# Two transformer layers in one kernel: spilling q and k of layer 1 one by one, and other places in the slots

## The reference, cut to what matters

```python
x = L0_attn_query
xn = _layernorm(x)
x = x + L0_attn(xn) + L0_ffn(xn)      # 16 heads of 128, causal mask; gated gelu FFN in float8
xn = _layernorm(x)
x = x + L1_attn(xn) + L1_ffn(xn)      # 16 heads of 16, no mask; Hadamard-rotated silu FFN, hidden 1024

# L1_attn:
q = (x @ Wq + bq).reshape(b, l, 16, 16)
k = (x @ Wk + bk).reshape(b, l, 16, 16)
v = (x @ Wv + bv).reshape(b, l, 16, 16)
a = softmax(einsum('blhd,bLhd->bhlL', q, k) / 16)
out = einsum('bhlL,bLhd->blhd', a, v).reshape(b, l, 256) @ Wo + bo
```

## Time and profile before

| | |
|---|---|
| median of 3 runs | 989.36 us |
| the profiled execution: its time, its span | 987.0 us, 985.2 us |
| mean granted TensorE clock | 0.934 |
| busy: PE, DVE, ACT, POOL | 84%, 76%, 70%, 48% |
| a batch in the middle, in TensorE's windows | 95 to 97 us |

### The profile page before, as it was taken

How to read it: one execution, slowest core, us unless ns; L and a number is a source line. 1 busy time by engine, 2 the same in 40 slices (tenths; PEclk the granted TensorE clock), 3 DMA queues, 4 the chain that set the end, 5 groups by cost and what they waited for, 6 DMA issues and landing times.

```text
span 985.2 us, 21114 instructions
## 1 busy us (share of the span) xinstructions
PE 828.4 (84%) x7054; PEld 610.3 (62%) x7120; DVE 745.0 (76%) x2028; ACT 691.2 (70%) x1973; POOL 469.6 (48%) x734
## 2 busy tenths in 40 slices
PE   3456538999899999999899999999999999897564
PEld 1123225787677777777677777777777777665342
DVE  6988847766778877787778777877787887775584
ACT  2555616556678788877777888788778877785573
POOL 1443333313236655555555455556555555456342
PEclk9676769999999999999999999999999999999795
DMA  9544321212234344645464554455436454644454
GB/s 334 182 139 128 107 93 45 52 42 42 46 93 105 76 104 116 108 81 107 100 106 76 109 108 105 76 121 100 104 76 134 87 100 76 127 81 92 107 108 106
DMA packets 283178, 100.96 MB, mean 102 GB/s; under 512 B 241344, under 2 KB 281024, under 8 KB 281920
## 3 DMA queue, kind: packets, MB, share of 16 engines
q1 hardware_dynamic: 280368, 97.27, 44.3%
q10 hardware_dynamic: 2704, 2.36, 0.7%
HBM read 30.38 MB, written 10.49 MB: 41 GB/s over the span
## 4 chain that ended last, share of the span: by engine, by line
PE 52%; DVE 15%; SPq 8%; ACT 4%; issue 3%; DMA 3%; POOL 0%; POOLq 0%; DVEq 0%; ACTq 0%
PE ps L665 32%; PE ps L714 7%; SPq L1268 4%; PE ps L814 3%; PE ps L797 3%; PE ps L690 3%; DVE arena L659 2%; DVE arena L658 2%; DMA arena<-scratch_qk 2%; DVE arena L997 2%; DVE nb L1004 2%; SPq L1242 2%; ACT arena L873 2%; PE ps L823 1%; PE ps L799 1%
## 5 line engine op out<-in xcount | busy, mean ns | idle before, releaser
L659 DVE SCALAR_TENSOR_TENSOR arena<-ps,bqk,arena 128x256 bf16<-128x256 f32 x416 | 187.3, 479 | 71.2 <-ACT arena L654 70.1
L665 PE MATMUL ps<-arena,wqkv 128*128 128x256 bf16 x1728 | 215.5, 275 | 6.5 <-PEq L210 6.5
L654 ACT ACTIVATE arena<-ps,bqk 128x256 bf16<-128x256 f32 x416 | 179.4, 466 | 33.6 <-PE ps L665 23.1
L1172 POOL TENSOR_SCALAR arena<-arena,rc 128x128 f32<-128x128 f32 (+1 forms) x256 | 106.3, 428 | 184.0 <-DVE rc L1020 184.0
L665 PEld LDWEIGHTS ps<-arena,wqkv 128*128 128x128 bf16 x1728 | 161.7, 98 | 46.2 <-issue 28.1
L873 ACT ACTIVATE arena<-arena,nb 128x128 f32<-128x128 f32 (+1 forms) x256 | 114.3, 447 | 100.2 <-DVE nb L997 100.1
L1179 POOL TENSOR_SCALAR arena<-arena,rc 128x256 f32<-128x256 f32 x256 | 119.8, 483 | 84.9 <-DVE rc L1024 84.5
L1163 POOL TENSOR_TENSOR arena<-arena 128x512 bf16<-128x512 f32 x107 | 123.9, 1158 | 74.1 <-ACT arena L653 74.1
L653 ACT ACTIVATE arena<-arena 128x384 bf16<-128x384 f32 (+1 forms) x256 | 135.6, 568 | 13.6 <-POOL arena L1179 6.9
L873 ACT ACTIVATE arena<-ps,nb 128x256 f32<-128x256 f32 x256 | 118.8, 474 | 19.2 <-DVE arena L658 10.3
L714 PE MATMUL ps<-wo,arena 128*128 128x256 bf16 x768 | 106.5, 275 | 15.9 <-DVE arena L659 15.6
(11 more groups left out here) (98 smaller groups left out, 1279.6 us busy)
## 6 DMA issues: line engine op xcount, KB each, us to landing
arena<-scratch_qk SPq DMA_DIRECT2D x96, 64.0 KB, 2.2
arena<-arena SPq DMA_TRANSPOSE x256, 2.7
scratch_qk<-arena SPq DMA_DIRECT2D x32, 128.0 KB, 2.0
arena<-in_x SPq DMA_DIRECT2D x4, 512.0 KB, 8.8
arena<-in_w_gating SPq DMA_DIRECT2D x2, 1024.0 KB, 7.0
arena<-in_w_q SPq DMA_DIRECT2D x2, 1024.0 KB, 8.8
scratch_xT<-arena ACTq DMA_DIRECT2D x8, 256.0 KB, 6.5
arena<-in_w_k SPq DMA_DIRECT2D x2, 1024.0 KB, 6.4
```

Of the source, the lines that this page charges most:

```text
L654: return nc.scalar.activation(out, in_, ACT.Identity, bias=bias)
L659: return nc.vector.scalar_tensor_tensor(out=out, in0=in_, scalar=bias, in1=hi, op0=ALU.add, op1=ALU.subtract)
L665: last = nc.tensor.matmul(out, lhsT, rhs, start=(n == 0), stop=(n == len(steps) - 1))
L1172: last = nc.gpsimd.tensor_scalar(v, v, rc0[:, n % 4, i:i + 1], 1.0, ALU.mult, ALU.mult)
```

## The change

Six edits, all in the order of the slots' work or in who waits for what.

1. `spill` and `stack` take q (w = 0) and k (w = 1) one by one, with semaphores of their own. q is spilled in +8 and stacked in +9, k spilled in +9 and stacked in +10 (before: both spilled in +9 and stacked in +10).
2. In SP's slot they stand ahead of the turning DMAs, not behind them.
3. TensorE and ScalarE do transpose_x1 and the pieces behind `proj_v0` and `up_gate`, VectorE the low parts of both behind `v0_low` and `hidden`.
4. The v piece moves from +10 to +11.
5. VectorE's `variance` stands behind `max_0` and `o0_low` in its slot, not ahead.
6. ScalarE's high copy of q (or k) waits for the spill of q (or k) of the batch before alone.

```diff
-            return start1(b) + ((7, 8, 10)[w] if b < LASTB else 6)
+            return start1(b) + ((7, 8, 11)[w] if b < LASTB else 6)
...
                 if h == 0:
-                    pe.wait_ge(stacked[b % 2], 192 * (b // 2 + 1))
+                    for w in range(2):
+                        pe.wait_ge(stacked[w][b % 2], 96 * (b // 2 + 1))
...
@@ pe_program, the slot loop
+                if v_in(s) is not None:
+                    proj_v0(v_in(s))
+                for n in hidden_in[s]:
+                    up_gate(n, s)
                 for b in turns_in[s]:
                     transpose_x1(b)
                 for n in pieces_in[s]:
                     proj_qkv1(n)
-                if v_in(s) is not None:
-                    proj_v0(v_in(s))
-                for n in hidden_in[s]:
-                    up_gate(n, s)
...
@@ act_program
-                        act.wait_ge(spilled[(b - 1) % 2], 64 * ((b - 1) // 2 + 1))
+                        act.wait_ge(spilled[w][(b - 1) % 2], 32 * ((b - 1) // 2 + 1))
...
@@ dve_program, the slot loop
-                for b in ln_in[s]:
-                    variance(b)
                 if 0 <= s - 1 < NG0:
                     max_0(s - 1)
                 if 0 <= s - 4 < NG0:
                     o0_low(s - 4)
+                for b in ln_in[s]:
+                    variance(b)
...
-                for b in turns_in[s]:
-                    x1T_low(b)
-                for n in pieces_in[s]:
-                    qkv1_low(n)
                 for b in x1_in[s]:
                     x1_sum(b)
                 if v_in(s) is not None:
                     v0_low(v_in(s))
                 for n in hidden_in[s]:
                     hidden(n)
+                for b in turns_in[s]:
+                    x1T_low(b)
+                for n in pieces_in[s]:
+                    qkv1_low(n)
...
@@ sp_program
-            def spill(b):
-                sp.wait_ge(qkv1_lo, 3 * b + 2)
+            def spill(b, w):
+                sp.wait_ge(qkv1_lo, 3 * b + w + 1)
                 if b:
-                    sp.wait_ge(stacked[(b - 1) % 2], 192 * ((b - 1) // 2 + 1))
...
+                    sp.wait_ge(stacked[w][(b - 1) % 2], 96 * ((b - 1) // 2 + 1))
+                for a in range(2):
+                    sp.dma_start(scratch[w, a].rearrange("(m p) t -> p m t", p=P),
+                                 qk1[:, a, w, :, :]).then_inc(spilled[w][b % 2], 16)
+
+            def stack(b, w):
+                sp.wait_ge(spilled[w][b % 2], 32 * (b // 2 + 1))
                 upto(sp, s1_ps, H1 * (b - 1))
...
             for s in range(SLOTS):
+                for n in pieces_in[s - 1]:
+                    if n % 3 < 2:
+                        spill(*divmod(n, 3))
+                for n in pieces_in[s - 2]:
+                    if n % 3 < 2:
+                        stack(*divmod(n, 3))
                 if 0 <= s - 2 < NG0:
                     turn0(s - 2)
```

More of the change, by code:

```diff
@@ L630, in build @@
         turned1 = [sem(f"turned1_{i}") for i in range(RPT1)]
-        rows_ready, spilled, stacked = ([sem(f"{n}{i}") for i in range(2)] for n in ("rows_ready", "spilled", "stacked"))
+        rows_ready = [sem(f"rows_ready{i}") for i in range(2)]
+        spilled, stacked = ([[sem(f"{n}_{w}{i}") for i in range(2)] for w in "qk"] for n in ("spilled", "stacked"))
         stored = sem("stored")
@@ L973, in act_program @@
                     exp_1(n)
+                if v_in(s) is not None:
+                    v0_high(v_in(s))
+                for n in hidden_in[s]:
+                    gate_tanh(n)
                 for b in turns_in[s]:
@@ L977, in act_program @@
                     qkv1_high(n)
[L978 to L981, removed]
                 fold(s)
@@ L1250, in load_tokens @@
                              ).then_inc(cur_ready[b % 2], 16)
-            def spill(b):
-                sp.wait_ge(qkv1_lo, 3 * b + 2)
+            def spill(b, w):
+                sp.wait_ge(qkv1_lo, 3 * b + w + 1)
                 if b:
-                    sp.wait_ge(stacked[(b - 1) % 2], 192 * ((b - 1) // 2 + 1))
[L1256 to L1262, removed]
-                upto(sp, s1_ps, H1 * (b - 1))
[L1264 to L1270, removed]
+                    sp.wait_ge(stacked[w][(b - 1) % 2], 96 * ((b - 1) // 2 + 1))
[4 more added lines that the diff above has]
+                sp.wait_ge(spilled[w][b % 2], 32 * (b // 2 + 1))
+                upto(sp, s1_ps, H1 * (b - 1))
+                for r, a in enumerate(((0, 0, 1), (0, 1, 0))[w]):
+                    for par in range(2):
+                        row = 64 * par + HD1 * r
+                        sp.dma_start((qs, ks)[w][row:row + HD1, b % 2, :, :],
+                                     scratch[w, a].rearrange("(s e d) t -> e d s t", e=2, d=HD1)[par]
+                                     ).then_inc(stacked[w][b % 2], 16)
             def store(b):
@@ L1288, in sp_program @@
                     load_rows(b - 1)
[L1289 to L1294, removed]
                 for n in y_in[s - 1]:
```

## The result

| | before | after |
|---|---|---|
| median of 4 runs, us | 989.73 (988.39 to 990.41) | 958.84 (957.28 to 959.41) |
| ratio, 95% interval | | 0.9702 (0.9681 to 0.9722) |
| profiled execution: time, span, us | 987.0, 985.2 | 958.63, 956.8 |
| mean granted TensorE clock | 0.934 | 0.937 |

What follows compares the result with a forecast made beforehand. TensorE was taken to bound the middle batches, its waits costing their full length. Gains of 23.7 us in the middle and 6.7 in the last batch, 30.4 in all, gave 959.0 us, range 954 to 971.

Steps and rivals of the forecast that it cites:

- rival A: Whole kernel: all gains come as summed, 959 us, own range 955 to 964; chance 0.61.
- Edits 1 and 2: Middle batches: stacking DMAs issued earlier in SP's queue end TensorE's stack waits, gain 11.5 us, bounds 0 and 11.5.
- the slow clock's 3.3: Middle batches: the slower TensorE clock behind two stalls above 2.3 us goes with them, gain 3.3 us.
- Rival C: Stack waits: late through transfers, not place in SP's queue, so most of that gain is missing; 979 us, chance 0.07.
- Edits 3 and 4: Middle batches: waits ahead of x1's transposes (+6) and the v piece (+10) go, gains 3.6 and 2.7 us.
- the new wait in +9: Slot +9, ahead of project_out0: edit 3 adds about 0.17 us per batch, bounds 0 and 0.5; 1.0 over six.
- Edit 5: Slot +4: variance behind o0_low shortens project_out0's wait, gain 4.1 us over six batches, bounds 0 and 5.6.
- the 0.1 that was to come back a slot later: Slot after +4: about 0.1 us of edit 5's gain per batch lost again, VectorE having little idling to make up.
- batch 0: First batch: without scores1 or down as cover loses about 0.9 us, gets 0.4 back at its stack wait: -0.5.
- The last batch: Last batch: stack right behind SP's sixth turning DMA, 0.7 from slot +5; second exp gains 6.7 us, bounds 4 and 8.4.
- B: Whole kernel: new waits take a good part, 1 us in each of six batches and more; 970 us, chance 0.25.
- D: SP's queue in +9 and +10: turn0 gets behind spill and stack, misses attend0; slower, 1007 us, chance 0.05.

Runs made afterwards that it cites:

- z_sp_alone: Kernel before with edits 1, 2 and 6 alone, each turning DMA replaced by three plain copies that don't turn; 973.43 us, ratio to before 0.9862.
- m_port2: Small separate kernel: three kinds of VectorE instruction alone, then each beside a GpSimd add of two SBUF inputs; one execution of 72.16 us.
- z_last_old: z_after with the last batch's x1 transpose and its high and low parts ahead of up_gate again; 964.15 us, ratio to before 0.9769.
- z_after: The changed kernel with each turning DMA replaced by three plain DMAs copying the same bytes unturned; 967.36 us, ratio to before 0.9799.

## Why the prediction was right, and where it was not

The forecast of 959.0 met 958.84, and rival A came about. That the two agree to 0.2 us is partly luck. The span was forecast at 954.8 and came out at 956.8: the middle gave 3.2 us more than said and the last batch 5.2 less. And the median of before lay 2.7 above its profiled execution and that of after only 0.2, where the forecast carried 2.4 over, which makes up the 2.0.

**Edits 1 and 2: right.** All 11.5 us of stack waits went, and the slow clock's 3.3 with them: the longest idle time left in the middle is 0.9 and the granted clock 1.00. Slots +9 to +11 ran as worked out but for the stack of q, which took 3.81 us (half of 5.74 forecast), that of k taking 2.90; the margin at the scores came out at almost 4 us, and turn0 was never late. z_sp_alone shows that these edits, with edit 6, suffice. Rival C is refuted: the stacking DMAs take a median of 2.2 us to land before and after. Of the rule of the Trainium skill in "DMA: Bandwidth & Descriptors", section "Issuing engines are not separate DMA queues", that issue is usually small beside the DMA, the rows agree for one DMA (0.48 beside 2.2 to land). It doesn't carry over to twelve in a row, which hold SP for 5.74: the transfers are the same as before, only their place in the queue of issues has changed, and the waits are gone.

**How the terms are measured.** The list of the earlier trace rows gives the idle time between two records. That leaves out short waits, and where a record is missing it counts work as waiting. So the terms are measured here from the start of one instruction to the start of the next, against the same pair where nothing waits.

**Edits 3 and 4: right, and the new wait in +9 came.** Ahead of the transposes the wait had cost 0.77 us by this measure (0.60 in the list) and ahead of the v piece 0.61 (0.45), so the two gave 4.6 and 3.7 for 3.6 and 2.7. The new wait in +9 is not in the list, but it is there. VectorE's o0_low of after, TensorE's project_out0 in +9 and +10, and the weight load of the first:

```profile
452.31 0.48 DVE L660 SCALAR_TENSOR_TENSOR arena<-ps,bqk,arena 128x256 bf16<-128x256 f32 x1
```

```profile
451.30 1.48 PE L666 MATMUL ps<-arena,wqkv 128*128 128x256 bf16 x12
452.84 0.83 PE L716 MATMUL ps<-wo,arena 128*128 128x256 bf16 x6
...
456.88 1.48 PE L666 MATMUL ps<-arena,wqkv 128*128 128x256 bf16 x12
458.20 0.82 PE L716 MATMUL ps<-wo,arena 128*128 128x256 bf16 x6
```

```profile
452.84 0.55 PEld L716 LDWEIGHTS ps<-wo,arena 128*128 128x128 bf16 x6 [0.34 <-DVE arena L660]
```

o0_low ends at 452.79 and project_out0 starts at 452.84, 1.54 us after the product ahead of it. In +10 it is 1.32, so 0.22 is lost, and it is 0.22 or 0.23 in each of the six batches: 1.4 us where I had 0.17 each and 1.0.

**Edit 5: right in +4, 4.7 for 4.1.** The weight loads ahead of project_out0 in +4, before and then after:

```profile
425.28 0.10 PEld L669 LDWEIGHTS ps<-zeros 128*128 128x128 bf16 x1
426.50 0.55 PEld L714 LDWEIGHTS ps<-wo,arena 128*128 128x128 bf16 x6 [1.11 <-DVE arena L659]
```

```profile
422.19 0.55 PEld L716 LDWEIGHTS ps<-wo,arena 128*128 128x128 bf16 x6 [0.34 <-DVE arena L660]
```

A matmul on zeros stands ahead of project_out0 there, in both kernels. In the trace of before its record is missing in +4, so the 0.94 of the earlier trace rows holds some 0.2 us of work; z_sp_alone, where nothing of edit 5 is in and the record is there, lists 0.72. From the start of the product to that of project_out0 it took 2.43 us before (424.07 to 426.50) and takes 1.65 after (420.55 to 422.20): 0.78 less, what variance had held VectorE for. A little wait stays, as said: o0_low ends at 422.15 and project_out0 starts at 422.20. Only the 0.1 that was to come back a slot later did not.

Moving variance also shortened it. Its last instruction and the GpSimd instruction beside it, before:

```profile
424.91 0.59 DVE L1086 TENSOR_SCALAR ve<-mv 128x2 f32<-128x2 f32 x1
...
424.81 0.68 POOL L1184 TENSOR_TENSOR arena<-arena 128x256 bf16<-128x256 f32 x1 [1.58 <-DVE arena L1067]
```

The same two of after:

```profile
422.33 0.17 DVE L1088 TENSOR_SCALAR ve<-mv 128x2 f32<-128x2 f32 x1
...
421.28 0.67 POOL L1186 TENSOR_TENSOR arena<-arena 128x256 bf16<-128x256 f32 x1 [1.58 <-DVE arena L1069]
```

Before, the 128x2 instruction started beside GpSimd's and took 0.59 us; after, GpSimd's had ended at 421.95, and it took 0.17. Its median over eight batches went from 586 to 170 ns, and m_port2 shows the same stretching by itself. In +4 that changes nothing, for a stretched instruction holds VectorE like a long one. It may be why the 0.1 did not come back; no run shows that.

The sum of the middle then closes: 11.9 for the stack by this measure, 3.3 for the slow clock, 4.6, 3.7 and 4.7, less 1.4 in +9, is 26.8, against 26.9 measured. That leaves 0.1 for batch 0, where I had a loss of 0.5. So the middle was under-sized by 3.2, mostly because the list shows each wait some 0.1 to 0.2 too short.

**The last batch: right in its mechanism, wrong in one step.** The failed step is "Another 0.7 comes from slot +5, where up_gate now fills the 0.63 that the transposes waited". That wait did go, but slot +5 lost 3.0 us: the scores of slot 132 come 26.86 us earlier than before, the pieces (908.82 before, 884.95 after) only 23.87. I had followed the transposes to what they wait for, and not to who waits for them. Right behind them stands attend1, which takes the bank BK_M when x1T_low has let it go. Before, the twelve matmuls of up_gate lay between and covered ScalarE and VectorE; now they lie ahead and cover nothing. z_last_old shows it: the old order in that slot gives 3.65 us back up to the first stacked scores, 1.9 of them by the start of the pieces. z_sp_alone, with the new queue and the old order, has no wait ahead of attend1. How much of the 2.81 is the order and how much the long cast no run tells apart; the cast's excess is 1.1. In the middle batches the same order costs nothing, as attend1 isn't in slot +6 or +7 there.

The rest went as worked out. SP's sixth turning DMA ended at 893.64, 22.9 earlier than before, where 23.9 were left after slot +5; the stack followed at once, and the scores came 7.6 us after its start (7.5 forecast):

```profile
892.40 1.24 SPq L1244 DMA_TRANSPOSE arena<-arena  x1
893.73 5.74 SPq L1268 DMA_DIRECT2D arena<-scratch_qk  x12
```

ScalarE answers to the earlier trace rows as said, its high copy waiting for the turning DMA that now stands behind the stack:

```profile
902.39 0.63 ACT L654 ACTIVATE arena<-arena 128x512 bf16<-128x512 f32 x1 [2.39 <-DMA arena<-arena]
...
903.82 0.47 ACT L875 ACTIVATE arena<-ps,nb 128x256 f32<-128x256 f32 x1
```

That exp is 28.9 earlier than in the earlier trace rows: 26.9 from the middle and 2.0 here, for 6.7 forecast. Of the 4.7 missing, 3.7 is slot +5 and 0.9 lies between the pieces and that turning DMA: it is the slower clock around the new wait, at which the first 24 matmuls of the pieces took 3.72 us instead of 2.79. z_last_old, without that wait, has them at 2.79. Another 0.5 goes between here and the end, 28.4 in all.

**The rivals.** B did not come: the only new wait in the middle is that of 0.23 in +9, and the batches take 91.3. C is refuted. D did not come either, but z_after shows how near it stands: with 0.6 us more of SP's time per turn and a landing some 0.5 later, waits for turned weights appear, half of them in a slot that D named.

**Left open:** what one by one and what ahead (edits 1 and 2) are worth apart, variance or the v piece alone, and rows_after a slot later, which might take the GpSimd instruction away from the cast. None of these was measured, and neither was the kernel with edits 3 to 5 alone.

## What to carry to other kernels

When twelve small DMAs and a few urgent ones share one in-order queue, count the queue's time per issue, and put what can go early ahead of what waits. When a step is moved ahead of its cover, look not only at what it waits for but at the next user of the buffer or bank that it frees, in every stage where it stands: the order of the transposes that was free in six batches cost 3 us in the last, and 0.9 more through the slower clock around the wait. And size a short wait from start to start of the same instructions: a list of idle stretches left out 0.2 us six times here and counted a missing record as waiting.

## What the runs showed of the hardware

Each of these VectorE instructions, when it started while a GpSimd tensor_tensor on SBUF was running, ended only with it or up to 0.3 us after: a 128x256 cast took 1.01 us instead of 0.29, a scalar_tensor_tensor with two SBUF inputs 1.14 instead of 0.42, and a tensor_scalar of 128x2 elements 0.97 instead of 0.17; in the kernel 1.41 instead of 0.29 and 0.59 instead of 0.17. It doesn't hold for every pair: in after, VectorE's two tensor_scalar of `normalise` (from 875.85) took 0.91 us together though two GpSimd tensor_scalar ran from 876.03 to 877.10.

"SBUF — State Buffer" of the Trainium skill, section "SBUF: two separate sides", has the two engines share a pair of ports that one instruction holds for its whole length, and counts a VectorE instruction with two SBUF inputs among those that need it, against a GpSimd instruction that reads SBUF. The rows of m_port2 agree. I had expected the scalar_tensor_tensor to keep its time.

A turning DMA that goes straight out holds SP for 1.21 to 1.26 us (medians of the two kinds) and each of twelve stacking DMAs for 0.48 (5.74 in all), while three plain DMAs of the same bytes as one turn hold it for 1.76 to 1.83. In this change the time that the queue is held decided, not that of the landing, which is the same before and after.

Idle stretches of TensorE of 2.35 and 2.78 us were followed by the lower clock: the same instructions took 5.76 and 5.75 us behind them and 4.09 behind one of 1.83. In the last batch the lower clock made 24 matmuls take 3.72 us instead of 2.79.
